# The residual behind the scan: from an add on VectorE to a product on TensorE and a copy on ScalarE

## What is computed

```python
x = x + xattn(layernorm(x), ctx)     # 16 heads over 2048 context rows, then a projection
x = x + attn(layernorm(x), ...)      # the scan: returns residual + out
x = x + ffn(layernorm(x), ...)       # 2 shared and 8 routed experts, top 2 of 8
```

```python
residual = x                                   # the layer-normed x
xn = x * rsqrt(mean(x * x) + 1e-8) * norm_w
u, z, g = split(xn @ W_in + b_in, 3)
ut, dt = tanh(u @ W_x + b_x), sigmoid(z @ W_dt + b_dt)
h = gated scan over the tokens: h[t] = (1 - dt[t]) * h[t-1] + dt[t] * ut[t]
out = (h * sigmoid(g)) @ W_out + b_out
return residual + out
```

## Time and profile before

| what | before |
|---|---|
| median of three runs | 524.77 us (524.31 to 525.30) |
| the profiled execution's own time | 521.97 us |
| its span, first to last instruction | 520.1 us |
| TensorE busy | 481.5 us, 93% |
| VectorE busy | 406.1 us, 78% |
| ScalarE busy | 330.3 us, 64% |
| GpSimd busy | 274.4 us, 53% |
| mean granted TensorE clock | 0.976 of full speed |

### The profile page before, as it was taken

How to read it: one execution, slowest core, us unless ns; L and a number is a source line. 1 busy time by engine, 2 the same in 40 slices (tenths; PEclk the granted TensorE clock), 3 DMA queues, 4 the chain that set the end, 5 groups by cost and what they waited for, 6 DMA issues and landing times.

```text
span 520.1 us, 16104 instructions
## 1 busy us (share of the span) xinstructions
PE 481.5 (93%) x6883; PEld 343.3 (66%) x6883; DVE 406.1 (78%) x614; ACT 330.3 (64%) x367; POOL 274.4 (53%) x262
## 2 busy tenths in 40 slices
PE   3988789899999999999989988998999999999994
PEld 3455556566767676667666667645787878787642
DVE  3767667688787788878758888787899999999426
ACT  3376477577676767776576256464788988888310
POOL 0449587999999999998960303461010111010051
PEclk9699969999999999999999999999999999999998
DMA  6999948899888899779989120278999999996144
GB/s 221 238 302 233 259 116 242 245 293 264 225 228 257 255 262 274 234 190 315 346 316 362 45 82 2 63 261 330 408 346 418 418 420 418 416 417 280 42 121 141
DMA packets 29822, 133.99 MB, mean 258 GB/s; under 512 B 6452, under 2 KB 6708, under 8 KB 18996
## 3 DMA queue, kind: packets, MB, share of 16 engines
q1 hardware_dynamic: 26072, 120.91, 70.9%
q0 software_dynamic: 3680, 12.06, 6.3%
HBM read 96.77 MB, written 11.01 MB: 207 GB/s over the span
## 4 chain that ended last, share of the span: by engine, by line
PE 50%; DVE 25%; issue 9%; DMA 8%; POOL 4%; ACT 2%; SPq 1%; DVEq 0%; ACTq 0%; POOLq 0%
PE bank L1089 8%; DVE ws L822 8%; PE bank L1149 8%; DVE mx L756 6%; PE bank L1134 6%; PE bank L1158 6%; DMA wst<-in_ffw 5%; POOL ps L672 3%; PE bank L1224 3%; PE bank L1289 2%; PE bank L1288 2%; PE bank L1287 2%; PE bank L1166 2%; DVE hf L1005 1%; DMA wst<-kl 1%
## 5 line engine op out<-in xcount | busy, mean ns | idle before, releaser
L756 DVE TENSOR_REDUCE mx<-bank 128x1 f32<-128x512 f32 x240 | 154.6, 686 | 53.5 <-PE bank L1089 51.7
L506 ACT ACTIVATE pt<-bank 128x1024 f32<-128x1024 f32 x128 | 124.5, 1023 | 54.7 <-PE bank L1134 48.5
L672 POOL TENSOR_TENSOR ps<-pt 128x512 f32<-128x512 f32 x120 | 150.5, 1282 | 0.0
L822 DVE SCALAR_TENSOR_TENSOR ws<-wst,ws 128x2048 f16<-128x2048 f32 x51 | 116.7, 2305 | 2.7 <-ACT ws L562 2.5
L562 ACT ACTIVATE ws<-wst 128x2048 f16<-128x2048 f32 x48 | 90.5, 1904 | 6.3 <-DMA wst<-in_ffw 6.3
L1302 PE MATMUL bank<-xt,ws 128*128 128x128 f16 x480 | 81.2, 219 | 0.9 <-DVE hf L1005 0.8
L1303 PE MATMUL bank<-xt,ws 128*128 128x128 f16 x480 | 81.2, 219 | 0.0
L1304 PE MATMUL bank<-xt,ws 128*128 128x128 f16 x480 | 81.2, 219 | 0.0
L713 POOL DMA_DIRECT2D ys_rows<-xn x15 | 8.2, 543 | 121.6 <-ACT xn L629 121.6
L648 POOL TENSOR_TENSOR kl<-kt,kh 128x512 f16<-128x512 f32 x58 | 66.4, 1168 | 10.9 <-ACT kh L452 10.9
L1149 PE MATMUL bank<-pt,v 128*32 128x128 f32 x2048 | 69.0, 275 | 0.3 <-issue 0.2
(11 more groups left out here) (187 smaller groups left out, 765.6 us busy)
## 6 DMA issues: line engine op xcount, KB each, us to landing
wst<-in_ffw SPq DMA_DIRECT2D x51, 1024.0 KB, 10.7
kt<-in_keysT SPq DMA_DIRECT2D x16, 1024.0 KB, 6.5
v<-in_vals SPq DMA_DIRECT2D x16, 1024.0 KB, 8.7
kstk<-kh SPq DMA_DIRECT2D x88, 128.0 KB, 4.7
kstk<-kl SPq DMA_DIRECT2D x44, 128.0 KB, 3.2
wst<-kh SPq DMA_DIRECT2D x40, 128.0 KB, 4.5
xs_rows<-biases SPq DMA_DIRECT2D x15, 256.0 KB, 6.8
x_tok<-xs_rows POOLq DMA_DIRECT2D x15, 256.0 KB, 8.8
```

The lines of the kernel that those rows point to most:

```text
L506: act.activation(pt[:, n % 4, :, :, :].rearrange("p j a t -> p (j a t)"), bank[:, 2 * (n % 2):2 * (n % 2) + 2, :].rearrange("p j n -> p (j ...
L672: pool.tensor_tensor(ps2[:, n % 4, :, :], pt[:, n % 4, 0, :, :], pt[:, n % 4, 1, :, :], ALU.add)\
L756: dve.tensor_reduce(mx[:, a, q:q + 1], bank[:, 4 + k % 2, :], AX.X, ALU.max).then_inc(m_taken, 1)
L822: dve.scalar_tensor_tensor(ws[:, home_of(q), 1, m, :, :].rearrange("p c n -> p (c n)"), wst[:, q % 2, m, :, :].rearrange("p c n -> p (c n) ...
```

## The change

The sum is formed in PSUM. VectorE makes a float32 identity times 16 (`idw`). TensorE multiplies it with `x2` and so puts 16 times the residual into bank 4 + b; the two products of the scan's output are added on top. ScalarE copies bank / 16 to `x2`, and the add on VectorE is gone. Ten idle products are taken out, and four float32 products stand in the same part of TensorE's stream. In ScalarE's stream the first two copies stand ahead of the first root, the third and the fourth behind the first and the second root.

```diff
--- before.py
+++ after.py
@@ -108,6 +108,7 @@
     wout = sb("wout", [P, D], F32)
     cols = sb("cols", [P, 4], F32)
     eps = sb("eps", [P, 2], F32)
+    idw = sb("scaled_identity", [P, P], F32)
     gwt = sb("gwt", [P, C, E], F32)
     gbias = sb("gbias", [P, B, E], F32)
     iota = sb("iota", [P, E], F32)
@@ -259,6 +260,7 @@
     ut_done = sem("ut_done")
     y_done = sem("y_done")
     scan_out = sem("scan_out_ready")
+    idw_done = sem("scaled_identity_done")
     x2_done = sem("x2_done")
     ln3_var = sem("ln3_var")
     h3_done = sem("h3_done")
@@ -595,8 +597,16 @@
         act.wait_ge(g_ready, 3)
         act.activation(sg[:, :], bank[:, 1, :], ACT.Sigmoid, bias=cols[:, 1:2]).then_inc(sg_done, 1)
         split_first(2)
+        def take_residual(b):
+            act.wait_ge(scan_out, b + 1)
+            act.activation(x2[:, b, :], bank[:, 4 + b, :], ACT.Copy, scale=1.0 / WS).then_inc(x2_done, 1)
+
+        take_residual(0)
+        take_residual(1)
         for b in range(B):
             root(ln3_var, b + 1, b, b + 1)
+            if b + 2 < B:
+                take_residual(b + 2)
             if b == B - 1:
                 act.activation(r1[:, 2, 0:2], eps[:, :], ACT.Exp)
             if b > 0:
@@ -886,6 +896,7 @@
             dve.tensor_scalar(x2[:, b, :], x1[:, b, :], r1[:, 2, b:b + 1], r1[:, 1, b:b + 1], ALU.mult, ALU.add)\
                 .then_inc(x1h_done, 1)
         dve.wait_ge(wo_hi, 1)
+        dve.tensor_scalar(idw[:, :], idf[:, :], WS, None, ALU.mult).then_inc(idw_done, 1)
         dve.scalar_tensor_tensor(wo[:, 1, :], wout[:, :], WS, wo[:, 0, :], ALU.mult, ALU.subtract).then_inc(wo_lo, 1)
         split_low(0, 1)
 
@@ -919,10 +930,6 @@
                               xh[:, :, b * P:(b + 1) * P], ALU.subtract).then_inc(xl_done, 1)
 
         for b in range(B):
-            dve.wait_ge(scan_out, b + 1)
-            dve.wait_ge(x2p_done, b + 1)
-            dve.scalar_tensor_tensor(x2[:, b, :], bank[:, 4 + b, :], 1.0 / WS, x2[:, b, :], ALU.mult, ALU.add)\
-                .then_inc(x2_done, 1)
             dve.wait_ge(x2_done, b + 1)
             stats(x2, b, ln3_var)
             if b > 0:
@@ -1267,13 +1274,26 @@
             for _ in range(count):
                 pe.matmul(bank[:, n, 0:P], idf[:, :], idf[:, :], start=True, stop=True)
 
-        idle_products(4, 10)
-        pe.wait_ge(wo_lo, 1)
-        for b in range(B):
+        def residual(b):
+            pe.wait_ge(x2p_done, b + 1)
+            pe.matmul(bank[:, 4 + b, :], idw[:, :], x2[:, b, :], start=True, stop=False)
+
+        def scanned(b):
             pe.wait_ge(y_done, b // 2 + 1)
             for n in range(2):
-                mm = pe.matmul(bank[:, 4 + b, :], yst[:, b * P:(b + 1) * P], wo[:, n, :], start=(n == 0), stop=(n == 1))
+                mm = pe.matmul(bank[:, 4 + b, :], yst[:, b * P:(b + 1) * P], wo[:, n, :], start=False, stop=(n == 1))
             mm.then_inc(scan_out, 1)
+
+        pe.wait_ge(idw_done, 1)
+        residual(0)
+        residual(1)
+        residual(2)
+        pe.wait_ge(wo_lo, 1)
+        scanned(0)
+        scanned(1)
+        residual(3)
+        scanned(2)
+        scanned(3)
 
         def up(n, it, tokens=slice(0, T), last=True, parts=range(2)):
```

## The result

The changed kernel's seven runs lie from 520.38 to 521.93 us, median 521.11; those of the kernel before, with four more made beside them, from 521.92 to 525.30, median 524.64. The medians differ by 3.5 us where 1.59 were forecast, and 521.11 lies outside the stated range of 522.3 to 524.4. The ratio on record is 0.9944, with a 95% interval from 0.992 to 0.9969, wholly under 1; it is not the quotient of the two medians (0.9933) and stands for 2.9 us. The profiled execution of the changed kernel took 521.11 us, its span 519.3. In all that follows four runs are left out as belonging to a slower state, each over 1.5% above the fastest run of its kernel beside it: 527.61, 529.29 and 530.91 us of the kernel before, and 525.31 of both_third.

What follows compares the result with a forecast made beforehand. No single engine bounds the whole; VectorE's chain from 300 to 321 us sets the fourth transpose. Gains of 0.16 and 1.43 sum to 1.59 us, so 524.77 - 1.59 = 523.2 us, range 522.3 to 524.4.

Steps and rivals of the forecast that it cites:

- The stretch: From VectorE's last operation on the scan's first half (the landmark) to the fourth transpose's start: 1.59 us gained.
- TensorE ahead of the scan: Three residual products, 0.86 us each, replace idle products from 304.71 and fit in the wait for the scan: cost 0.
- TensorE behind the scan: Scan products, fourth residual product and twenty idle rows bring TensorE to the first transpose at 312.64, not 312.80: 0.16 us gained.
- ScalarE: Two copies delay the table load to 309.58 and first root to 310.88; normed tile 0 is still ready 0.72 us early.
- The rule on the table switch: Ahead of ScalarE's first root: the skill's drain of about 1.38 us per switch would make the gain 0.9 us.
- Rival A: ScalarE's table switch costs some 1.4 us more than its row; gain 0.9 us, 523.9 us; chance 0.10.
- First to fourth transpose: The links between these transposes sum to 4.77 us instead of 6.20: 1.43 us gained.
- The operations off VectorE: Four adds leave VectorE's chain from 300 to 321 us: 2.9 us, the most the edit can give.
- What follows: Behind the stretch, the weight stream and full stretch of 385 to 470 us start earlier; all of 1.59 us is passed on.
- rival B: Earlier, but given back: dearer residual products take 0.8 us (524.0) or the full DMA stretch takes all (524.8); chance 0.14.
- D: Slower: TensorE's clock falls in the changed stretch; some 9 us more, about 532 us; chance 0.05.
- The signs in absolute time: Fourth transpose at about 317.4 us, and every later landmark and the last store 1.6 us earlier.

Runs made afterwards that it cites:

- both_third: Changed kernel with 3 idle products instead of 10 and the square root's table loaded early, repeated: median 521.29 us, ratio 0.9944, stretch 8.99 us.
- three_idle: Changed kernel with 3 idle products instead of 10 ahead of the first transpose, one profiled run: stretch 9.49 us against 10.10.
- table_early: Changed kernel with the square root's table loaded ahead of the copies and the weight tile's conversion moved later, one profiled run: stretch 10.09 us.
- copy_on_vector: Changed kernel with VectorE instead of ScalarE copying the bank out, one profiled run: stretch 11.74 us against 10.10.
- same_program: The kernel before, unchanged, timed against itself: median 523.79 us, ratio 1.002, stretch 11.75 us.
- tile_alone: The kernel before with the scaled identity's 512 bytes per partition allocated and never used: median 523.06 us, ratio 1.0018, stretch 11.75 us.
- tile_again: The kernel before with the unused tile in place of the scaled identity, repeated: median 522.82 us, ratio 0.9993, stretch 11.75 us.
- both_edits: Changed kernel with 3 idle products instead of 10 and the square root's table loaded early, 12 runs: median 519.83 us, ratio 0.9941, stretch 8.99 us.

## Why the prediction was right and wrong

**The stretch** held step by step: 1.65 us against 1.59, in all four profiles of the changed kernel (10.09 or 10.10), in both of the changed kernel with no tile moved (10.09), and in all five of the program before, two of them with the unused tile (11.75 or 11.76).

- *TensorE ahead of the scan*: six residual rows of 0.43 from 305.76, done in time, and the wait for the scan is still there with 0.37 us, where 0.5 was forecast. Cost 0, as said.
- *TensorE behind the scan*: the first transpose 5.39 us behind the landmark, as forecast (312.64 - 307.25), against 5.55. The ten idle products hold it: three_idle takes 0.61 us off by removing seven. With the fourth product moved, the gain was 0.28, 0.33 expected.
- *ScalarE*: first statistics 1.83 behind the landmark (forecast 1.85), table load 2.31 (2.33), first root 3.60 (3.63). The load is exposed on ScalarE, but the first transpose doesn't wait for it, as TensorE comes there later still; table_early confirms that it costs nothing here. With three idle products instead of ten the transpose waits for its input, and there the early load is worth 9.49 - 8.99 = 0.50 us.
- *The rule on the table switch*: the Trainium skill ("ScalarE: Activation LUTs", What ACT_TABLE_LOAD costs) has about 1283 ns of load and about 1380 ns of drain for every switch. The load agrees: 310.60 + 1.28. The drain doesn't appear: the root starts at 311.89, 0.01 us behind the load, and the load 0.03 us behind the copies (309.49 + 1.08). By the figures of the Trainium skill the gain would have been an estimated 0.9. Rival A is refuted.
- *First to fourth transpose*: 4.71 us against 4.77 forecast and 6.20 before. The 0.06 are a hand-over: a transpose group that follows other products without a gap took 0.60 us to its end, not 0.66. VectorE's wait ahead of the first low part was 0.53, where about 0.7 was forecast.
- *The operations off VectorE*: copy_on_vector gives all of it back, 11.74.
- *What follows*: the expert stages moved as a block (200.9 against 201.1). The part of rival B in which the DMA stretch takes the gain is refuted, as is its dearer product (rows of 0.43). D did not happen: the clock was granted in full from 305 through 321 us. (Its price was summed wrongly: 24 us of work from 304.7 end at 328.7, 11 behind the forecast 317.4, which is 534 us and not 532. Nothing else rests on it.)
- *The signs in absolute time* did not come: the fourth transpose was forecast at 317.4 and the end 1.6 us earlier, and they came at 318.39 and 0.8 us earlier, as this execution reached the scan 1.04 us later.

**The step that failed** is the last one, "the median of the runs is 2.8 above it, at 524.77, and gives 524.77 - 1.59". It took the median of three runs, 1 us apart, as the time of this kernel, let the range rest on the doubts of the sum alone, and put the error of a measurement at 0.2%. The kernel before has a much wider spread: over 130 runs, 519.14 to 527.14 us, median 523.30, standard deviation 1.5. The sets differ as well: beside the changed kernel the median of seven runs was 524.64, in the four later sets 522.2 to 523.7. Three runs, or seven of one set, say little about the centre at the 0.2% that mattered. The sign was on the table: the profiled execution at 521.97 lay 2.3 us below the lowest of the three. From 523.30 the same sum gives 521.7, and the 35 runs of the changed kernel have a median of 520.99 (518.17 to 522.93).

So of the 1.9 us that the first timing has beyond the stretch, 1.3 are its base (524.64 against 523.30). Whether these came by chance or with the chip of that first set isn't on record. That leaves about 0.7 us by the medians of all runs, 0.6 and 0.3 by the two averages of ratios, that the stretch doesn't hold. No stretch of the profile shows it: neither the tail, equal within its spread (200.4 to 201.9 us in the profiles of both), nor the part ahead of the scan, where only the small operation at 299.36 is new and the landmark comes no earlier than in the program before. But these are single executions, and the last section shows that they need not lie where the timed runs do. How much of it is the error of the measure, and whether a part is real, stays open.

**Where the spread comes from.** In the seventeen profiles of this case the landmark lies between 306.89 and 311.88 us, 5 us apart; the part behind the fourth transpose varies by 1.5 us (200.4 to 201.9), and the stretch, kernel by kernel, by 0.01. So most of the spread of the profiles is made ahead of the scan. VectorE's landmark row in same_program, in tile_alone and in tile_again, whose instructions are the same up to there:

```profile
307.09 0.42 DVE L906 TENSOR_TENSOR scan_y<-scan_a,scan_y 64x256 f16<-64x256 f32 x1
```

```profile
311.47 0.42 DVE L907 TENSOR_TENSOR scan_y<-scan_a,scan_y 64x256 f16<-64x256 f32 x1
```

```profile
311.88 0.42 DVE L907 TENSOR_TENSOR scan_y<-scan_a,scan_y 64x256 f16<-64x256 f32 x1
```

Almost all of that difference is there when the attention is half done. VectorE makes sixteen reciprocals of its denominators. The first one comes earlier in the slower program (50.72 us in tile_alone, 53.19 in same_program), the second already 3.4 us later (75.39 and 71.98). The seventh starts at 152.51 in same_program and at 156.53 in tile_alone, and from there to the landmark it takes 154.58 and 154.94. The granted clock falls and returns at other moments. The stretches of same_program, then of tile_alone (us, busy by engine, clock, DMA share, GB/s):

```profile
30.00:35.00 5.00, 4.46 (x21) 2.00 (x20) 3.44 (x6) 4.21 (x6) 1.31 (x2) 0.50 1.03 275
...
50.00:55.00 5.00, 4.90 (x82) 3.38 (x83) 4.87 (x9) 4.12 (x6) 3.99 (x5) 1.00 0.98 266
```

```profile
30.00:35.00 5.00, 3.89 (x52) 2.19 (x54) 4.86 (x8) 5.00 (x7) 1.32 (x2) 1.00 1.04 239
...
50.00:55.00 5.00, 2.13 (x57) 1.75 (x50) 3.13 (x7) 1.66 (x2) 5.00 (x6) 0.96 1.03 265
```

At 30 to 35 us the slower one even has the better clock, 1.00 against 0.50; at 50 to 55 its TensorE is busy for 2.13 us instead of 4.90, while the DMA engines are full in both. Why it differs was not tried. The tiles' place doesn't settle it: the two changed kernels in which no tile moves reach the landmark at 311.24 and 310.83 us, later than the four in which the tiles do (307.92 to 308.87).

## What to carry to other kernels

Before an operation is moved off the busiest engine, write down when each of its neighbours would come to the next hand-over by its own stream; the gain is what the slowest of them allows. Here TensorE's own filler held the first transpose, and only with seven idle products taken out, and the exposed table load then moved as well, did the stretch shrink by another 1.1 us (over the 23 runs of both_edits and both_third the median is 520.02 us, 3.3 under the 523.30 of before, for a stretch 2.76 us shorter; on the one chip that ran it beside the changed kernel, the further 1.1 us did not show). To measure a change of 0.3%, compare the stretch in single profiles from a landmark inside, where it agrees to 0.01 us; this says what the stretch gives, and only many runs say what the whole gives. And take the spread of a base time from many runs, never from three; a profiled execution that lies far off their median is a fourth sample, not an offset to add.

## What was not expected of the hardware

- One program's times spread over 1.5% (519.14 to 527.14 us), while 11.75 us inside it repeat to 0.01.
- The profiled executions of one program can agree with each other and lie off its centre. The three of the kernel before have the landmark at 307.09, 307.23 and 307.25 us, on at least two chips, and took 521.25 to 521.97 us where the median is 523.30. The two with the unused tile have it at 311.47 and 311.88 and took 526.25 and 527.08, but their 24 runs have a median of 522.86. A single profile of each would have said that the unused tile costs 4 us; its ratios, 1.0018 and 0.9993, show no cost. The two of the changed kernel with no tile moved took 524.85 and 524.02, with a median of 521.92 over 24 runs. It isn't a rule: the four of the changed kernel go from 520.86 to 522.69, and the two of both edits took 518.73 and 521.29.
- Two copies out of PSUM, back to back on ScalarE, took 1.08 us together (309.49) and a single one 0.58 (312.09), so the second starts 0.50 us behind the first. On VectorE the same copy takes 0.73 us until the statistics that read it can start (310.30 to 311.03 in copy_on_vector); this includes the hand-over, the 0.50 doesn't.
